# A four-layer conditioned residual stack on one core: GpSimd's steps in another order

## The reference, cut

```python
x = x + (einsum('bnh,boh->bno', x, W0[subject]) + b0[subject])        # 8 subjects
x = x + rotate_pairs(x, amplitudes ** dt, frequencies * dt)           # pairs of tokens
x = x + (einsum('bsd,bdh->bsh', x, W2[category]) + b2[category])      # 64 categories
h = relu(einsum('bsh,bha->bsa', x, W1[language]) + b1[language])      # 9 languages used, 128 wide
y = x + einsum('bsa,bah->bsh', h, Wup[language]) + bup[language]
x = x + (y - mean(y)) * rsqrt(var(y) + eps) * gamma[language] + beta[language]
```

## Time and profile before

| | us |
|---|---|
| median of three runs | 1190.81 |
| profiled execution, its own time | 1182.38 |
| its span, first to last instruction | 1180.6 |
| TensorE busy | 1119.9 |
| VectorE busy | 958.4 |
| GpSimd busy | 827.6 |
| ScalarE busy | 791.9 |

### The profile page before, as it was taken

One profiled execution on the slowest core, in us unless ns is written; L12 is line 12 of the kernel. 1 busy time (PEld: TensorE's weight loads), 2 busy tenths in 40 slices (PEclk: granted clock), 3 DMA queues, 4 the chain that ended last, 5 costly groups with the idle time before them and its releaser, 6 DMA issues.

```text
span 1180.6 us, 29959 instructions
## 1 busy us (share of the span) xinstructions
PE 1119.9 (95%) x6040; PEld 937.4 (79%) x6040; DVE 958.4 (81%) x1344; ACT 791.9 (67%) x1828; POOL 827.6 (70%) x794
## 2 busy tenths in 40 slices
PE   4999999998999998999997999989998999999996
PEld 2688878887888886888886888878887888788885
DVE  5888888887888787788886888878887888778886
ACT  2667777766677675677766677667675767667774
POOL 5777677776777566777776677767776677767774
PEclk8899999999999998999998999989998999989999
DMA  8977876777787678768768876887688677868782
GB/s 273 393 244 243 264 271 216 239 253 243 247 252 250 210 252 274 244 215 256 241 212 285 254 238 210 255 279 224 223 258 276 210 250 250 276 210 252 245 255 89
DMA packets 96993, 290.18 MB, mean 246 GB/s; under 512 B 11422, under 2 KB 12062, under 8 KB 78972
## 3 DMA queue, kind: packets, MB, share of 16 engines
q1 hardware_dynamic: 95880, 287.46, 74.5%
q10 hardware_dynamic: 884, 0.42, 0.2%
HBM read 254.00 MB, written 33.84 MB: 244 GB/s over the span
## 4 chain that ended last, share of the span: by engine, by line
PE 51%; SPq 26%; issue 12%; DMA 5%; DVE 2%; POOL 1%; ACT 1%; ACTq 0%; POOLq 0%; DVEq 0%
PE ps_hT L974 6%; PE ps_l L905 6%; SPq L222 6%; PE ps_l L944 6%; PE ps_l L948 6%; PE ps_l L954 6%; PE ps_l L922 5%; PE ps_mix L933 5%; SPq L237 3%; DMA b_in<-b 3%; PE ps_l L909 3%; PE ps_l L916 3%; PE ps_x3T L964 3%; SPq L225 2%; SPq L240 2%
## 5 line engine op out<-in xcount | busy, mean ns | idle before, releaser
L767 DVE TENSOR_TENSOR w_lo<-w_in,w_hi 128x1024 fp32r<-128x1024 f32 x256 | 387.1, 1512 | 0.0
L552 ACT ACTIVATE w_hi<-w_in 128x1024 fp32r<-128x1024 f32 x256 | 257.2, 1052 | 132.1 <-PE ps_l L948 130.0
L461 POOL TENSOR_TENSOR x<-x,beta_sb 128x512 f32<-128x512 f32 x128 | 258.5, 2020 | 111.1 <-DVE ps_y L805 110.8
L424 POOL TENSOR_TENSOR w_in<-w_in,ident 128x512 f32<-128x512 f32 x128 | 171.4, 1339 | 121.1 <-DMA w_in<-W 117.7
L597 ACT ACTIVATE x3T<-ps_x3T,minus_bup 128x128 f32<-128x128 f32 x512 | 146.4, 367 | 66.8 <-PE ps_x3T L964 66.7
L792 DVE TENSOR_TENSOR x<-ps_l,b_in 128x512 f32<-128x512 f32 x128 | 88.5, 691 | 120.5 <-PE ps_l L954 120.3
L431 POOL TENSOR_TENSOR x_lo<-x_in,x_hi 128x512 fp32r<-128x512 f32 x127 | 164.7, 1297 | 7.0 <-ACT x_hi L524 5.8
L905 PE MATMUL ps_l<-w_hi,x_hi 128*128 128x512 f32 x512 | 155.6, 427 | 3.6 <-ACT x_hi L524 2.1
L933 PEld LDWEIGHTS ps_mix<-mix,x 128*128 128x128 f32 x1024 | 127.1, 195 | 37.6 <-issue 37.6
L933 PE MATMUL ps_mix<-mix,x 128*128 128x128 f32 x1024 | 145.1, 286 | 7.3 <-DVE x L775 7.1
L974 PE MATMUL ps_hT<-x3T,w_in 128*128 128x128 f32 x1024 | 141.1, 282 | 9.5 <-ACT x3T L597 9.5
(11 more groups left out here) (110 smaller groups left out, 1829.2 us busy)
## 6 DMA issues: line engine op xcount, KB each, us to landing
w_in<-W SPq DMA_DIRECT2D x128, 1024.0 KB, 5.9
x_in<-xT SPq DMA_DIRECT2D x128, 256.0 KB, 4.6
w_in<-W SPq DMA_DIRECT2D x128, 256.0 KB, 2.6
out<-yb SPq DMA_DIRECT2D x128, 256.0 KB, 5.1
b_in<-bias_rows SPq DMA_DIRECT2D x127, 256.0 KB, 5.5
w_in<-W0T SPq DMA_DIRECT2D x8, 1024.0 KB, 5.1
wup_sb<-Wup SPq DMA_DIRECT2D x1, 2560.0 KB, 11.9
gamma_sb<-gamma SPq DMA_DIRECT2D x1, 2560.0 KB, 12.2
```

The source lines that it names most:

```text
L424: pool.tensor_tensor(diagonal_of(w2_in[s % WB]), diagonal_of(w2_in[s % WB]), ident[:, :].unsqueeze(1).broadcast_to([P, C, P]), ALU.add).th ...
L461: pool.tensor_tensor(x3[s % X3B][:, :], x3[s % X3B][:, :], beta_sb[:, bass.ds(here, D)], ALU.add)\
L552: act.activation(w2_hi[:, halves[n]], w2_in[s % WB][:, halves[n]], ACT.Copy).then_inc(w2_hi_made, 1)
L767: dve.tensor_tensor(w2_lo[:, half], w2_in[s % WB][:, half], w2_hi[:, half].bitcast(fp32), ALU.subtract).then_inc(w2_lo_made, 1)
```

## The change

Only GpSimd's loop and its end are touched. Step s now runs: the wait for both halves of w2_lo of s; beta of s-2 (before: of s-1, after fold_w2); h_lo of s-1; x_lo of s+2; the remaining Wup parts (in step 0 alone); fold_w0 of s+3, if its subject is new (before: last); a new wait for the first half of w2_lo of s+1; fold_w2 of s+2; the inverse deviation of s-1 (before: of s-2, at the head of the step, which is the same place for steps in a row). The wait for the beta table moves from step 1 to step 2. Behind the loop beta of sample 126 is added, behind the variance of sample 126.

```diff
             for s in range(B):
-                if s >= 2:
-                    inverse_deviation(s - 2)
+
                 if s < LAST - 1:
                     pool.wait_ge(w2_lo_made, 2 * s + 2)
+                if s == 2:
+                    pool.wait_ge(beta_loaded, 16)
+                if s >= 2:
+                    add_beta(s - 2, language_offset(pool, s - 2))
                 if s >= 1:
                     rest_of_h(s - 1)
                 if s < LAST - 1:
                     rest_of_x(s + 2)
-                    fold_w2(s + 2)
                 if s == 0:
                     for n in range(3, len(wup_parts)):
                         rest_of_wup(n)
-                if s == 1:
-                    pool.wait_ge(beta_loaded, 16)
-                if s >= 1:
-                    add_beta(s - 1, language_offset(pool, s - 1))
                 if s < LAST - 2:
                     fold_w0(s + 3)
+                if s < LAST - 1:
+                    pool.wait_ge(w2_lo_made, 2 * s + 3)
+                    fold_w2(s + 2)
+                if 1 <= s < LAST:
+                    inverse_deviation(s - 1)
             rest_of_h(LAST)
             inverse_deviation(LAST - 1)
+            add_beta(LAST - 1, language_offset(pool, LAST - 1))
             add_beta(LAST, language_offset(pool, LAST))
             inverse_deviation(LAST)
```

## The result

| | before | after |
|---|---|---|
| median, on the same chips (6 runs each) | 1191.67 | 1209.74 |
| lowest and highest | 1188.68 to 1193.99 | 1205.07 to 1214.17 |
| profiled execution, its own time | 1182.38 | 1212.24 |
| its span | 1180.6 | 1210.4 |
| mean granted clock | 0.972 | 0.963 |

The ratio of after to before is 1.0147, with an interval of 1.0124 to 1.0169: the kernel became 18 us slower. Lines behind 480 are numbered 4 higher in the kernel after (L824 is L828, L984 is L988, L771 there is the old L767, L556 the old L552).

What follows compares the result with a forecast made beforehand. TensorE, busy 95%, was taken as the bound, losing 55.8 us mostly in seven W0 samples. Terms 3.3 + 15.4 - 2.6 - 2.0 - 1.5 + 1.2 = +13.8 on 1190.81 gave 1204.6, range 1192 to 1216.

Steps and rivals of the forecast that it cites:

- Six W0 samples, 2.56 each: Between W0's landing and L824, fold_w2 and beta become unhidden, 1.28 us each, in six samples: +15.4 us.
- The first one, +3.3: The first W0 sample, with no idle time before its fold, becomes like the second: +3.3 us, bounds 0.5 and 4.6.
- Ordinary samples, 0: In undisturbed samples beta is in time for L824 by 0.28 us: 0, bounds 0 and 0.1 per sample.
- slower still: Rival: beta misses L824 in every sample through the register load or a longer L767: 1216 to 1228 us; chance 0.13.
- fold_w2 behind w_lo, 0: fold_w2 takes beta's place beside L767's second half, which is held as before: saves nothing, costs nothing.
- Given back, -2.6: SyncE catches up in the second W0 sample; six late samples from 402 us and the third W0 gain: -2.6 us.
- Single samples, -2.0: Samples where GpSimd's fold or beta held up w_lo's first half are freed, as the fold now waits: -2.0 us.
- Start, -1.5: At the start Wup parts no longer stand behind fold_w2, so L767's first half isn't held: -1.5 us.
- End, +1.2: At the end beta of sample 126 stands behind rstd, and the last sample's chain hangs on L824: +1.2 us.
- given back everywhere: Rival: SyncE's queue is the true pace and fewer late loads repay each TensorE stall: +1 to +4, about 1193; chance 0.14.
- Faster: Rival: beta no longer contends with w_lo and W0 lands before its fold comes up: 1180 to 1188 us; chance 0.09.

Runs made afterwards that it cites:

- the fold-last kernel: The changed kernel with fold_w0 of s+3 again last in GpSimd's loop, behind fold_w2 and the variance: 1213.55 us, ratio 1.0179.
- the kernel with the fold of W2 late: The kernel before with only fold_w2 moved, behind beta of s-1 and a wait for w_lo's first half: 1185.48 us, ratio 0.9987.
- The single moves: The kernel before with one move each: fold_w0 ahead of fold_w2 (1205.35 us), beta late (1200.66 us), fold_w2 late (1185.48 us).
- the kernel with beta late: The kernel before with only beta moved: beta of s-2 behind both halves of w2_lo: 1200.66 us, ratio 1.0081.
- the old order written out: The kernel before with SyncE's 128 steps written out instead of looped over twelve: 1142.93 us, ratio 0.9635.
- the two kernels that issue W0 early: The kernel before and the changed kernel, each with SyncE issuing W0 one sample earlier: 1174.63 us (ratio 0.9844) and 1178.21 us (0.9857).

## Why the prediction was right, and where it wasn't

1204.6 was predicted, in 1192 to 1216; 1209.74 was measured. The step that carried it holds: the fold of W0 waits for a landing that GpSimd doesn't set, and what stands between it and L824 is paid by TensorE. By its waits TensorE pays nearly all of it in front of h_lo (13.7 us before, 41.9 after), which the prediction names in half a sentence, and not in front of x1, by which it was worked out.

- **Six W0 samples, 2.56 each.** The chain from the fold's end to L828 grew by 2.40 to 2.93, 2.64 in the mean of all seven. Over seven that is 18.5 us (predicted 3.3 + 15.4 = 18.7). L828 comes 3.74 to 4.11 behind the fold's end, where about 3.65 was predicted. The fold of W2 and beta are as priced (1.26 each and the 0.20 of beta's register load in the timeline).
- **The first one, +3.3.** It lost 5.43 after 2.38: +3.05.
- **Ordinary samples, 0.** The period stayed 8.43. But the room of 0.28 us was 0.1: of the register load ahead of beta 0.20 is not hidden. The prediction's "nothing up to 1.0" was wrong on this point: the fold-last kernel exposed 0.91 and paid in 113 samples. The rival "slower still" was one load away, closer than its chance of 0.13 says.
- **fold_w2 behind w_lo, 0.** Shown alone: 0.9987.
- **Given back, -2.6.** This failed. The third W0 was indeed issued 0.6 us earlier against the work, but the late samples behind 402 stayed, 1.6 us of loss for 2.0. Elsewhere SyncE came later, not sooner: W0 was issued later against L988 by 0.7, 2.8, 2.1, 1.2, 0.9 and 3.3 us in the six others. Their sum less the 0.6 is about 10.3 us, and the W0 samples lost 77.3 - 47.7 - 18.5 = 11.1 us more than the chain explains. This is what the prediction lacked: it held W0's landing fixed ("its issue is SyncE's and not moved") and expected these samples to lose 60 to 66 us, not 77.3. It is as large as most of the difference between the profiled executions' 29.9 us and the medians' 18.1. I take it that how SyncE stands varies between executions and that the old kernel's profiled execution was a fast one. That is argued: only one execution of each has a trace. For it speaks the kernel with the fold of W2 late, whose chain is that of before and whose time is no longer: in its profiled execution (1189.03, 3.6 above its median) the W0 samples lose 58.1 us, 10.4 more than those of before. The single moves speak for it too, with W0 issued 6.0 to 7.3 us later in all. So it isn't shown that the new order makes SyncE later.
- **Single samples, -2.0.** Three of the four are gone, but eight that lose 0.2 to 0.3 came in their place: 2.2 us in all, nothing gained. What fell, by 1.1, is the loss of samples with a late W2.
- **Start, -1.5.** It didn't come. L988 of sample 2 starts at 68.20 (68.08 before), and TensorE still waits 1.63 us there, where L771 takes 3.43 us beside the two Wup parts:

```profile
38.33 6.70 POOL L447 TENSOR_TENSOR wup_sb<-wup_sb,wup_hi 128x1024 fp32r<-128x1024 f32 x2
...
42.68 3.43 DVE L771 TENSOR_TENSOR w_lo<-w_in,w_hi 128x1024 fp32r<-128x1024 f32 x1
...
46.77 1.19 PE L952 MATMUL ps_l<-w_hi,x2T_lo 128*128 128x512 f32 x4 [1.63 <-DVE x2T_lo L786]
```

- **End, +1.2.** Met: from L988 of sample 125 to the end 21.0 us, before 19.8, and L828 waits 1.61 for beta:

```profile
1202.99 0.75 DVE L828 SCALAR_TENSOR_TENSOR yb<-ps_y,rstd,x 128x512 f32<-128x512 f32 x1 [1.61 <-POOL x L461]
```

The sum of what was measured: 18.5 for the chain, 1.2 for the end, 0.1 at the start and -1.1 in the other samples make 18.7, beside 18.1 by the medians. It leaves out the 11.1 us by which the W0 samples lost more than the chain explains; with them it is 29.8, the difference of the two profiled executions. Of the 5.1 us between forecast and result, 0.9 is the median of before, which is 1191.67 over six runs and was 1190.81 over three. The rest is mostly the three gains that didn't come (-2.6, -2.0, -1.5), of which 1.1 did. The forecast's upper end of 1214 leaves out a bound that the prediction itself gives, 0.1 us in each ordinary sample or some 12 us; only the rival "slower still" carries it. Of the rivals, "given back everywhere" had the right suspect, SyncE's queue: stalls do bring it back into step, but it falls behind again within one or two loop ends. "Faster" fell with the waits on L418 and with the kernel with beta late, where w2_lo is relieved and nothing is gained. My own statement that the waits would come to 45 us was low (61.7); W0's later issue accounts for 10 of these 17.

**Open:** what sets how late SyncE stands. Its register load behind x's issue (L237, the flag of a new W0) takes longer (ns, shortest, median, longest; before, after, and the old order written out):

```profile
L237 SPq TENSOR_LOAD <-ids x127: 262/529/1114, 31.5 to 1141.7; - x127
```

```profile
L237 SPq TENSOR_LOAD <-ids x127: 262/718/1178, 32.2 to 1168.1; - x127
```

```profile
L237 SPq TENSOR_LOAD <-ids x127: 262/288/1212, 34.1 to 1097.7; - x127
```

A median of 718 ns for 529 fits the 0.1 us by which SyncE's step grew, but it doesn't hold throughout: with the fold of W0 last it is 563, and the step is as long as after the change (8.62). It was 573 to 670 with one move at a time. What holds the load up was not found out; SyncE's other loads aren't held up (L222: 270 ns in the median of 382, before). The Trainium skill (DMA: Bandwidth & Descriptors, Latency and other measured facts) gives a floor of about 600 ns for a `tensor_load`; the trace has 262 at the least and 288 in the median of the written-out kernel, so here the measurement decides against it.

Nor is the loop end explained. Measured is that it costs 4.6 us on SyncE, most of it right behind the branch, and that it goes when the steps are written out. The Trainium skill (Advanced Engine Details and Errata, ISA Cache) gives a sequencer's instruction cache two lines of 256 instructions; a body of twelve steps (47 recorded instructions each, 564 in all) that had to be fetched anew at each jump would agree with it, but no run here shows the cache, nor did I try a shorter body.

## What to carry to other kernels

Before a step that may wait for a DMA is moved forward in an engine's order, list what stands behind it up to the next value that the bottleneck needs: each of these steps was hidden while it was ahead of the wait, and is paid in full behind it (here 2 x 1.28 us, seven times). Read the waits for a transfer together with when it was issued: here the landing, and 43 us, hung on how the issuing engine's own loop was written, which showed as busy nowhere. And in a short chain count the register loads too: 0.9 us of them cost more than the wait that was removed for it.

## What the runs showed of the hardware

- The end of a loop of twelve steps on SyncE costs 4.6 us (5.7 to 6.1 between L312 and L295 instead of 1.25), nine times, and 2.8 to 3.2 of it lie right behind the branch; in the two kernels that issue W0 early it costs about 3.2. Written out, there is none, and each step is some 0.6 us shorter on SyncE as well: by both together the kernel of the old order went from 1186.18 to 1142.93.
- A register load takes 0.26 us at the least on SyncE. Most take 0.27 (L222), but the one behind x's issue (L237) has a median of 0.29 to 0.73 in these kernels and takes up to 1.3. On GpSimd a load can't be seen as busy time: it shows as "issue", 0.20 us ahead of beta behind rstd, 0.91 with a second load and a branch.
- GpSimd and VectorE hold each other up. Beta takes 2.00 us beside L767 and 1.30 elsewhere in the new order, and L767 takes 1.72 us beside beta and 1.22 in the kernel with beta late.
- The clock follows the stall. Windows of after around the second new W0 (stretch, length, busy PE PEld DVE ACT POOL, granted clock, DMA share, GB/s): full ahead of it, 0.61 in the four us in which TensorE did nothing, and 0.50, the lower of its two levels (1.2 of 2.4 GHz), in the next four, in which it went to work again. Before, it was 0.75 at that point.

```profile
283.00:287.00 4.00, 2.42 (x13) 1.70 (x11) 0.69 (x1) 0.00 (x0) 0.16 (x1) 1.00 0.99 268
287.00:291.00 4.00, 0.00 (x0) 0.00 (x0) 0.00 (x0) 1.65 (x2) 3.27 (x5) 0.61 0.96 382
291.00:295.00 4.00, 2.16 (x7) 1.68 (x8) 2.25 (x5) 2.00 (x4) 2.69 (x3) 0.50 0.29 83
```
